# Adding a group's node sums one turn sooner on VectorE, in a graph network with sorted edges

## What is computed

```python
edge_attr = swish(edge_attr_raw @ enc_W + enc_b)
for _ in range(4):
    e_in = concatenate([edge_attr, x[src], x[dst]])
    e_upd = layernorm(swish(e_in @ eW1 + eb1) @ eW2 + eb2, eg, ebeta)
    edge_attr = edge_attr + e_upd
    agg = segment_sum(edge_attr, dst, num_segments=3125)
    n_in = concatenate([x, agg])
    x = x + layernorm(swish(n_in @ nW1 + nb1) @ nW2 + nb2, ng, nbeta)
out = layernorm(x0 + x)
```

## Time and profile before

| | us |
|---|---|
| median of 3 runs | 2649.68 |
| lowest and highest run | 2647.38, 2649.91 |
| the profiled execution's own time | 2649.45 |
| its span, first to last instruction | 2647.7 |

### The profile page before, as it was taken

The page is one execution under the profiler, slowest core; times in us unless marked ns, Lnnn a source line. Parts: engine busy times, 40 slices in busy tenths (PEclk is TensorE's granted clock), DMA queues, the critical chain, the costliest instruction groups (busy, mean ns, idle before and its releaser), DMA issues.

```text
span 2647.7 us, 83245 instructions
## 1 busy us (share of the span) xinstructions
PE 2416.0 (91%) x27990; PEld 1867.3 (71%) x27990; DVE 2285.0 (86%) x6586; ACT 1969.2 (74%) x5343; POOL 1627.7 (61%) x1581
## 2 busy tenths in 40 slices
PE   2899999999978999999987999999987999999995
PEld 1477777777746777777765777777774777777774
DVE  5599999999865999999964999999984799999997
ACT  1588888888646888888845888888864888888874
POOL 0477666666107777777704777777721777777750
PEclk8899999999999999999998999999998999999998
DMA  2666666666337888878725888778834666666640
GB/s 78 192 195 196 197 190 194 195 190 194 103 125 207 247 244 243 249 246 245 230 90 176 243 249 243 244 242 249 246 127 144 197 195 196 198 199 197 195 133 25
DMA packets 380878, 512.86 MB, mean 194 GB/s; under 512 B 57676, under 2 KB 254418, under 8 KB 380440
## 3 DMA queue, kind: packets, MB, share of 16 engines
q1 hardware_dynamic: 305176, 301.81, 34.9%
q0 software_dynamic: 75264, 205.62, 28.7%
HBM read 389.35 MB, written 117.85 MB: 192 GB/s over the span
## 4 chain that ended last, share of the span: by engine, by line
PE 84%; issue 6%; DVE 4%; DMA 2%; POOL 2%; ACT 1%; DVEq 0%; ACTq 0%; SPq 0%; POOLq 0%
PE psum L1613 18%; PE psum L1643 18%; PE psum L1601 13%; PE psum L1674 7%; PE psum L1593 6%; PE psum L1625 5%; PE psum L1384 4%; PE psum L2077 3%; PE psum L1638 2%; POOL arena L1572 2%; PE psum L2116 2%; PE psum L2090 2%; PE psum L1655 2%; DMA arena<-node_tables,idx_all 2%; PE psum L1670 1%
## 5 line engine op out<-in xcount | busy, mean ns | idle before, releaser
L1572 POOL DMA_INDIRECT arena<-node_tables,idx_all x1568 | 1625.1, 1036 | 931.3 <-issue 427.1
L1739 ACT ACTIVATE arena<-psum 128x1024 f16<-128x1024 f32 x392 | 401.1, 1023 | 426.9 <-PE psum L1613 426.9
L1839 DVE SCALAR_TENSOR_TENSOR arena<-psum,arena 128x1024 f16<-128x1024 f32 x392 | 478.3, 1220 | 184.9 <-issue 84.3
L1643 PE MATMUL psum<-w_hi,arena 128*128 128x128 f16 x6272 | 589.3, 219 | 4.9 <-DVE arena L1839 3.3
L1643 PE MATMUL psum<-w_lo,arena 128*128 128x128 f16 x3136 | 545.5, 219 | 0.0
L1643 PEld LDWEIGHTS psum<-w_hi,arena 128*128 128x128 f16 x6272 | 498.3, 98 | 17.9 <-DVE arena L1839 4.3
L1613 PE MATMUL psum<-arena,w_hi 128*128 128x512 f16 x1568 | 470.3, 382 | 2.3 <-ACT arena L1785 2.3
L1601 PE MATMUL psum<-ident,arena 128*128 128x128 f16 x6272 | 418.5, 220 | 15.5 <-DMA arena<-node_tables,idx_all 15.2
L1761 ACT ACTIVATE arena<-psum 128x128 f32<-128x128 f32 x1568 | 412.7, 290 | 5.7 <-PE psum L1643 5.7
L1601 PEld LDWEIGHTS psum<-ident,arena 128*128 128x128 f16 x6272 | 385.3, 98 | 29.7 <-DMA arena<-node_tables,idx_all 21.0
L1740 ACT ACTIVATE psum<-psum 128x1024 f32<-128x1024 f32 x392 | 399.5, 1019 | 0.0
(11 more groups left out here) (174 smaller groups left out, 3253.7 us busy)
## 6 DMA issues: line engine op xcount, KB each, us to landing
state<-arena SPq DMA_DIRECT2D x294, 256.0 KB
arena<-state SPq DMA_DIRECT2D x294, 256.0 KB
arena<-node_tables SPq DMA_DIRECT2D x784, 64.0 KB
arena<-matrices SPq DMA_DIRECT2D x294, 128.0 KB
node_tables<-arena SPq DMA_DIRECT2D x100, 256.0 KB, 2.2
arena<-node_tables,idx_all POOLq DMA_INDIRECT x1568
arena<-rel_rows SPq DMA_DIRECT2D x98, 128.0 KB
matrices<-arena SPq DMA_DIRECT2D x98, 128.0 KB
```

The lines of the kernel that those rows point to most:

```text
L1572: pool.indirect_dma_start(out=rows[n % R][:, t, :], out_offset=None, in_=p_table, in_offset=bass.IndirectOffsetOnAxis(ap=idx_all[:, n % G1 ...
L1643: x = pe.matmul(ps_v(k2)[:, t * P:(t + 1) * P], h[k2][:, half, t * P:(t + 1) * P], w[:, half, :], start=False, stop=half == 1 and h is hl, ...
L1739: act.activation(hh[k2], ps_h(k2), ACT.Silu).then_inc(S("hh"), 1)
L1839: dve.scalar_tensor_tensor(hl[k2], ps_h(k2), 1.0, hh[k2], ALU.mult, ALU.subtract).then_inc(S("hl"), 1)
```

## The change

In `slot(n)` the register with the window's start is read at the head of the turn, now for group n-7 and not n-8, and the addition follows behind `low(n)`. A group's sums are so added one turn of DVE sooner. With that the last of the turns behind the groups is left out.

```diff
                 def slot(n):
-                    add_window(n - LAG - 4, window(n - LAG - 4))
+                    w = window(n - LAG - 3)
                     matrices_of(n + 2)
                     first_low(n + 1)
                     low(n)
+                    add_window(n - LAG - 3, w)
                     if n % 2:
                         root(n - 3, 0, 2)
                         for t in range(TPG):
...
                 for g in range(G1 + 4, G1 + 6):
                     slot(first + g)
                 update(1, nothing)
-                for g in range(G1 + 6, G1 + 8):
-                    slot(first + g)
+                slot(first + G1 + 6)
                 seed_chunk(NCH - 1)
```

## The result

| | before | after |
|---|---|---|
| median, us (4 runs each, same chip) | 2649.8 | 2623.84 |
| lowest and highest run | 2647.38, 2652.03 | 2620.42, 2630.66 |
| the profiled execution, us | 2649.45 | 2620.42 |
| its span, us | 2647.7 | 2618.7 |

The ratio is 0.9907, with a 95% interval of 0.9892 to 0.9922: the change takes 26 us off, 0.9%. The forecast was 2628 us. The same kernel, timed once more beside the last experiments, gave 2628.7 us against 2650.07 (ratio 0.992, 0.9903 to 0.9937).

The account below looks back on a forecast made before the run. The prediction took the loop through DVE's odd turn and late addition as the bound (10.81 us a pair), then POOL at 10.68: 132 pairs give 17 us, step ends 4, so 2649.45 - 21 = 2628 us; 8-in-10 range 2590 to 2656.

Parts of the forecast that it names:

- (a): TensorE before node sums L1674: addition ends some 4 us before needed, hole goes, TensorE alone needs 10.16 us a pair.
- (b): DVE behind the low half: new wait for sums of group n-7, covered by about 0.8 us, costed at nothing.
- (f): Ends of the four steps: 1 us gained in each, 4 in all; bounds a gain of 10, a loss of 8.
- (c): Node sums on TensorE next wait for low_new (L1900): cover 0.3 us, thin; with DVE's 9.99 still allows about 10.16 a pair.
- (d): POOL's gathers, stretched by DVE's two-input operations, set the pair at 10.68 us instead of 10.81; bounds 10.16 to 10.95.
- the first rival: POOL's gathers find other gaps, TensorE's 10.16 us a pair holds: 2559 us, chance 0.14.
- (e): Number of pairs that gain: 44 of 49 in each of three later steps, 132; first step costed at nothing.
- The sum: Whole kernel: 17 us from the pairs plus 4 from the ends, 21 off 2649.45, gives 2628 us.
- POOL follows: Gathers find other gaps and TensorE's 10.16 us a pair holds: 2559 us, chance 0.14.
- POOL takes all: POOL settles at the present pair of 10.81 us, the hole becomes a wait for gathers, only ends gain: 2645, chance 0.22.
- Slower: DVE's two-input operations shut POOL out more, TensorE pays late gathers: 10.95 us a pair, 2664 us, chance 0.12.

Follow-up runs that it names:

- the combined one: Kernel before, with the addition one turn sooner in odd turns only and low_new (L1900) ahead of the four scalings in odd turns: 2623.85 us.
- the thinned kernels: Kernel before and changed kernel, each without the fourth gather of a group in the three later steps, third tile multiplied twice: 2641.83 and 2565.26 us.

## Why the prediction was right, and where it was lucky

**What bounded the kernel before** was read rightly: the loop through DVE's odd turn and the late addition. Two runs show it from two sides: a quarter fewer gathers does nothing to the pair, and 0.11 us more in the odd turn comes out as 0.11 us in the pair.

**(a)** The hole goes, from 28 to 30 us a step to 4 to 6; undisturbed turns of 5.07 us show the 10.16 that TensorE alone wants. Right.

**(b)** The new wait was costed at nothing. Right in the steady part, where L1919 has no bracket. Only in the last turns of a step, which have no low half, does DVE stand, as (f) said: up to 2.96 us, here on DVE of after.

```profile
1327.67 0.29 DVE L1919 TENSOR_TENSOR agg_deg<-agg_deg,psum 128x128 f32 x1 [2.96 <-PE psum L1674]
```

**(c)** L1900 is late next, as said, and its cover is thin: 4 to 6 us a step remain in front of L1674. The row of after for the whole run puts 10.7 of 11.7 us of idle time down to L1900; 6.2 of them are three waits of 2.06 us at ends of steps, and 4.5 lie in the steady part (less than in the table, because the row counts from the modelled end). With L1900 out of the way the hole was gone and the wait for gathers about as large as before (16 to 18 us and not 15 to 17): the pair stayed with the gathers' pace, which that order made faster.

```profile
L1674 PE MATMUL psum<-arena 128*128 128x128 fp8e4 x3136 | 238.7, 219 | 11.7 <-DVE arena L1900 10.7
```

**(d)** POOL takes over, at 10.68 a pair; measured 10.60 to 10.69. This carried the forecast, and with fewer gathers the gain went on to 85 us, about the first rival's number (2559; 2565 measured, of which the missing gathers alone account for some 8 us, as in the kernel before). But the value was right by luck. I took 10.68, from the heads of the steps, as POOL's own pace under DVE's load and let it stand unchanged. Over the steady part of before the row above gives (360.2 + 105.4) / 346 x 8 = 10.77, again without a pause, so that POOL had some 0.05 us a pair in hand and not 0.13; with that pace kept, the change would have been worth some 132 x 0.05 + 4 = 11 us (my estimate from these rows). The row of after gives (358.4 + 106.6) / 350 x 8 = 10.63. So most of the 0.16 us a pair that the later steps gained came with a faster POOL, which the prediction had put at nothing, and the new pace happened to fall near 10.68. What part of it comes from the moved addition itself and what part from the shorter pair, no run separates. The pace is no constant of the load: in after, L1900 holds eight gathers for 0.39 us where it did for 0.67, and L1891 for 0.20 where it did for 0.05; the sum fell by 0.12. With the same operations in other orders, eight gathers exceed their 7.56 us by 0.49 to 0.80. My last sentence on what would make the prediction fail, the place of gathers against single operations, was the better description; the bounds 10.16 to 10.95 did hold all of it.

The Trainium skill (SBUF — State Buffer, section "SBUF: two separate sides") says that a DVE operation with two SBUF inputs and a GpSimd operation that reads SBUF get the shared ports in turn, the second blocked until the first is done. This trace agrees for gathers that start inside such an operation, and with PSUM as one input the block is gone (0.95 us beside L1893 in the kernel with L1891 from PSUM); it does not agree that a running gather blocks DVE: L1900 takes 0.685 us in after with a gather already under way (150 cases in the steady part) and 0.685 without (111).

**(e)** 132 pairs x 0.13 = 17 us were expected. Measured were 20.8 and 19.0 us in two executions, over 130.5 pairs; the size is right, but its source is mostly the change of POOL's pace, as said under (d).

**(f)** The ends gave 3.7 and 3.9 us for the 4 expected. The wait at the place of the earlier trace rows fell from 2.68 to 2.06 us, on the way named: from the addition to L1900.

```profile
1320.36 0.61 PE L1674 MATMUL psum<-arena 128*128 128x128 fp8e4 x8 [2.06 <-DVE arena L1900]
```

**The sum**: 21 us expected; 26 in the first comparison and 21.4 in the second.

**The rivals.** POOL follows: no, as long as L1891 and L1900 have two SBUF inputs. POOL takes all: no, 10.66 and not 10.81; but by POOL's pace in the steady part of before (10.77) it was nearer than 0.22 sounds. Slower: not in this kernel, but it was nearer than 0.12 sounds: its point of 10.81 us for eight gathers is passed by the kernel before with L1900 first (10.75 to 10.82, by their starts) and almost reached by the combined one (10.64 to 10.74), both with the same operations on DVE.

**Open**: which order of DVE's turn gives the fastest gathers cannot be told from these runs in advance. The two fastest full kernels, the change in odd turns only and the change with L1900 first, at 2602 and 2600 us, beat the changed kernel by 0.8 to 0.9%, and were found, not derived.

## What to carry to other kernels

When a stall is taken from the engine that sets the pace, look for the engine that was faster by the least: here POOL had half a percent to 1% in hand (10.77 or 10.68 of 10.81 us a pair), and it kept two thirds of what the stall's removal was worth (26 us came of the 77 that the thinned kernels differ by). Test it by thinning out that engine's work in both kernels: no gain before and a large one after shows the change of hands. And a rate that was measured under contention is a property of one order of instructions; for another order give it a range, and read it where the steps run steadily, not at their heads.

## What the runs showed of the hardware

**One point at which a gather can be held.** Of the gathers in before that start more than 0.05 us into L1900 (218) the median ends 0.82 us after that operation's end (0.81 to 0.83, except for the few that start in its last 0.1 us), up to 1.45 us long. Undisturbed they take 0.945. So they are held at one place, some 0.13 us behind their start; past it DVE doesn't touch them, nor they DVE. When both start within 0.05 us, DVE gives way a little: L1891 at 0.76 and not 0.69, with a gather of 0.95 beside it.

**A late gather can lower TensorE's clock.** Where TensorE had run ahead and waited 1.95 us for rows, its clock fell. Timeline of TensorE in after, then the granted clock in three stretches there (length, busy times, then PEclk as the third number from the end):

```profile
1195.01 1.89 PE L1601 MATMUL psum<-ident,arena 128*128 128x128 f16 x16 [1.95 <-DMA arena<-node_tables,idx_all]
1196.69 1.06 PE L1613 MATMUL psum<-arena,w_hi 128*128 128x512 f16 x2
1197.54 0.63 PE L1613 MATMUL psum<-arena,w_lo 128*128 128x512 f16 x1
```

```profile
1190.00:1196.00 6.00, 4.05 (x56) 3.51 (x54) 5.93 (x19) 4.42 (x12) 4.56 (x5) 0.91 0.84 263
1196.00:1202.00 6.00, 6.00 (x66) 4.52 (x64) 2.17 (x3) 3.00 (x5) 4.60 (x5) 0.81 0.79 240
1202.00:1208.00 6.00, 6.00 (x83) 4.98 (x81) 5.88 (x23) 5.35 (x21) 4.66 (x5) 1.00 0.53 153
```

The sixteen matmuls L1601 took 1.89 us and not 1.06, one of L1613 0.63 and not 0.38: the lower of the two levels (1.2 of 2.4 GHz) for about 3 us, after which it was granted in full again. Three such places are in the later steps of after's profile (near 1195, 2140 and 2312 us, with waits of 1.95, 2.80 and 2.72 us), with pairs of 14.0 to 14.8 us around them; the steady part of before has none, and neither has that of the second profile of after. Not every such wait does it: 1.98 us in that second profile, and 2.10, 1.91 and 1.88 us in the kernel with the addition ahead of L1849, left the clock at its upper level. What such a place costs in the end is not shown: POOL goes on without a pause there, pairs behind it run at 10.15 to 10.3 us until TensorE waits for gathers again, and the second profile, without any, has pairs of 10.70, 10.67 and 10.64 all the same. That the pairs of two executions differ by up to 0.07 us shows how much the gathers' pace itself moves.
